# Both stages in one program: attention of the first images inside the convolution's last image, and a token stage on pairs of images

## The reference, cut to what matters

```python
def reference(x, ...):                      # x: (8, 16, 16, 64), float32
    x = x + deformable_conv(group_norm(x))  # 8 groups, 9 taps, bilinear samples, then out @ op_w
    t = x.reshape(8, 256, 64)               # tokens
    n = layer_norm(t)
    q, k, v = n @ Wq.T + bq, n @ Wk.T + bk, n @ Wv.T + bv
    t = t + softmax(q @ k.T / 8) @ v        # within an image
    n = layer_norm(t)
    g = softmax(n @ gate_w + gate_b)        # 16 experts, the two largest kept, made to sum to 1
    y = [(silu(n @ w1[e]) * (n @ w2[e])) @ w3[e] for e in range(16)]   # 64 -> 128 -> 64
    return t + sum(g[e] * y[e] for e in range(16))
```

## Time and profile before

| | us |
|---|---|
| median of 3 runs | 456.4 (455.93 to 458.94) |
| the profiled execution's own time | 459.05 |
| its span, first to last instruction | 457.2 |
| PE at work in the span | 410.0 |
| DVE | 335.2 |
| ACT | 259.5 |
| POOL | 141.3 |

### The profile page before, as it was taken

The page is one execution under the profiler, slowest core; times in us unless marked ns, Lnnn a source line. Parts: engine busy times, 40 slices in busy tenths (PEclk is TensorE's granted clock), DMA queues, the critical chain, the costliest instruction groups (busy, mean ns, idle before and its releaser), DMA issues. The chain is left out here.

```text
span 457.2 us, 9731 instructions
## 1 busy us (share of the span) xinstructions
PE 410.0 (90%) x3276; PEld 232.0 (51%) x3276; DVE 335.2 (73%) x730; ACT 259.5 (57%) x571; POOL 141.3 (31%) x172
## 2 busy tenths in 40 slices
PE   1689999999999999999998457989999999999995
PEld 0543343433534335343332345867677776767663
DVE  3479967789777897777889346768777686868652
ACT  2683645746457464574610154676767677685752
POOL 2263223243232422324200164123242333324322
PEclk9979999999999999999999655799999999999997
DMA  8068886938559385583860330000000000000000
GB/s 258 3 155 218 215 222 148 229 89 227 163 122 231 91 226 158 117 239 86 226 162 1 141 134 0 2 0 2 2 0 14 3 0 14 1 2 1 11 3 11
DMA packets 28409, 44.91 MB, mean 98 GB/s; under 512 B 6864, under 2 KB 11088, under 8 KB 27984
## 3 DMA queue, kind: packets, MB, share of 16 engines
q1 hardware_dynamic: 28368, 44.39, 37.6%
HBM read 6.11 MB, written 0.52 MB: 15 GB/s over the span
## 5 line engine op out<-in xcount | busy, mean ns | idle before, releaser
L663 DVE TENSOR_TENSOR prod<-ps_t,a_rep 128x1024 f32<-128x1024 f32 x128 | 152.0, 1219 | 34.5 <-PE ps_t L363 32.3
L363 PE MATMUL ps_t<-b,vt 32*128 32x512 f32 x512 | 74.7, 650 | 1.9 <-DVE prod L663 1.9
L769 POOL TENSOR_TENSOR a<-a,mask 128x512 f32<-128x512 f32 (+1 forms) x40 | 47.0, 1178 | 83.7 <-ACT a L523 81.4
L383 PE MATMUL ps_d<-prod,keep 128*32 128x512 f32 x512 | 69.0, 611 | 0.3 <-DVE prod L663 0.2
L1223 POOL TENSOR_TENSOR total<-total,share 128x256 f32<-128x256 f32 x56 | 40.9, 730 | 86.9 <-DVE share L1117 86.5
L304 PEld LDWEIGHTS ps_m<-om_r,sel 128*128 128x128 f32 x193 | 29.0, 187 | 75.3 <-ACT mask L501 28.2
L1101 DVE TENSOR_TENSOR hidden<-ps_h,gated 128x256 f32<-128x256 f32 x128 | 51.4, 415 | 3.7 <-ACT gated L1316 2.8
L1316 ACT ACTIVATE gated<-ps_h 128x256 f32<-128x256 f32 x128 | 47.8, 387 | 7.5 <-PE ps_h L1436 1.1
L304 PE MATMUL ps_m<-om_r,sel 128*128 128x256 f32 x193 | 49.3, 334 | 0.0
L1117 DVE TENSOR_TENSOR share<-ps_yf,factor 128x256 f32<-128x256 f32 x56 | 23.7, 423 | 30.4 <-issue 12.8
L1310 ACT ACTIVATE factor<-ps_yf 128x256 f32<-128x256 f32 x64 | 24.6, 385 | 37.3 <-PE ps_yf L1471 37.3
(11 more groups left out here) (151 smaller groups left out, 671.3 us busy)
## 6 DMA issues: line engine op xcount, KB each, us to landing
a_rep<-a SPq DMA_DIRECT2D x128, 256.0 KB, 4.7
a_rep<-a SPq DMA_DIRECT2D x32, 128.0 KB, 2.8
w_f<-in_w SPq DMA_DIRECT2D x2, 1024.0 KB, 5.8
start<-in_start SPq DMA_DIRECT2D x1, 1344.0 KB, 7.8
x_turned<-in_x_turned SPq DMA_DIRECT2D x1, 512.0 KB, 3.8
t_tok<-in_x SPq DMA_DIRECT2D x1, 512.0 KB, 9.4
w<-in_w SPq DMA_DIRECT2D x1, 512.0 KB, 7.6
select_f<-in_select SPq DMA_DIRECT2D x1, 512.0 KB, 8.4
```

The source lines that it names most:

```text
L363: mm = pe.matmul(out, vt[par][r, v % 2, :, :, :].rearrange("p j y c -> p (j y c)"), b[par][r, pair_taps(v // 2), :].rearrange("p t x -> p ...
L383: mm = pe.matmul(ps_d[r, :], fold[:, v % 2, :], p, start=v == 0, stop=False, skip_group_check=True)
L663: dve.tensor_tensor(p[:, :, :], t[:, :, :], a_rep[par][:, ms, pair_taps(v // 2), :].rearrange("p m t x -> p m (t x)"), ALU.mult).then_inc( ...
L769: pool.tensor_tensor(v, v, mask[(PAIRS * par + k) % 2][:, 0:wide, :], ALU.mult).then_inc(a_done, 1)
```

## The change

- One function, one block: the SBUF of the convolution that is free before its last image (`early`) is given to the tokens' tiles, and the expert weights are loaded there. `early_free(eng)` stands before that on SP, ACT, DVE and POOL.
- The last image's `sample` and `weight` use two double banks of `ps_t` instead of three (`ring=2`); the third is `ps_bc`.
- Each engine calls `tokens(at, half)` twice per batch of the last image and twice per duet. It runs the steps due there: `due` gives the couple `c` (two images, 512 tokens) whose first place is `first` for couple 0 and `8 (c - 1) + later` for the others. Places -10 to -2 are the batches of the last image, -1 what follows them, 0 to 31 the duets.
- Expert passes have 512 columns: 32 duets, four couples. `expert_output` adds eight duets up in PSUM (`ps_y`). The shares are no longer spread by a matmul: `portions` (DVE) to `turn_portions` (PE) to `copy_portions` (ACT), then `share_out` on SP writes them to DRAM and reads them back with 128 copies (`factor`, four transfers of 1 MB per couple). POOL multiplies them into the output of `silu` (`weigh`), and DVE's `hide` comes after it.
- The first layer norm's last step moves from DVE to ACT (`apply_norm`), and `turn_sum` is four transposes, followed by two additions.

Core of the diff:

```diff
+def due(at, half, first, later):
+    for c in range(COUPLES):
+        if (at, half) == (first if c == 0 else (DUETS * (c - 1) + later[0], later[1])):
+            return c
+    return None
...
+        def early_free(eng):
+            eng.wait_ge(weighted, WPI * (IMAGES - 1))
+            eng.wait_ge(b_done, PAIRS * (IMAGES - 1) + FIRST_B)
+            eng.wait_ge(vt_ready, IMAGES)
+            for halves in a_filled:
+                for half in halves:
+                    eng.wait_ge(half, 16 * 2 * IMAGES)
...
+        LAST_JOBS = [("om", 0), ("om", 1), ("rep", 0), ("out", 0)]
+        LAST_JOBS += [("rep", r) for r in range(1, len(REPS))] + [("turn", 0)]
...
+            early_free(sp)
+            for w, name, arrived in ((w_f[0], "w1", w1_in), (w_f[1], "w2", w2_in), (w3, "w3", w3_in)):
+                sp.dma_start(w[:, :, :], d[name].rearrange("p (e h) -> p e h", e=EXPERTS)).then_inc(arrived, 16)
+            def share_out(c):
+                sp.wait_ge(p_copied, c + 1)
+                sp.dma_start(board[c], dispatch[:, :]).then_inc(p_out, 16)
...
+                if c > 1:
+                    sp.wait_ge(weighed, EXPERTS * (c - 1))
+                sp.wait_ge(p_out, 16 * (c + 1))
+                for g in range(4):
+                    e = slice(PIECE * g, PIECE * (g + 1))
+                    sp.dma_start(factor[c % 2][g], board[c, e].unsqueeze(0).broadcast_to([P, PIECE, WIDE]))\
+                      .then_inc(factor_in[g], 16)
...
-            def sample(v, i, par):
+            def sample(v, i, par, ring=TRING):
...
-                if positive(WPI * i + 2 * v - 1):
-                    pe.wait_ge(weighted, WPI * i + 2 * v - 1)
+                ahead = 0 if ring == 2 and v else 1
+                if positive(WPI * i + 2 * v - ahead):
+                    pe.wait_ge(weighted, WPI * i + 2 * v - ahead)
...
+            def product_1(u):
...
+                if u < 2:
+                    pe.wait_ge(weighted, WPI * IMAGES)
+                else:
+                    pe.wait_ge(silu_done, u - 1)
+                for w, first in ((w_h[0], True), (w_l[0], False)):
+                    mm = pe.matmul(ps_h1[u % 2][:, :], w[:, e, :], xf[c % 2][:, :], start=first, stop=not first)
...
+            def product_2(u):
...
+                    pe.wait_ge(hidden_done, u - 1)
...
+            def expert_output(p):
...
+                pe.wait_ge(hidden_done, 2 * (p + 1))
+                for k in range(2):
+                    u = 2 * p + k
+                    mm = pe.matmul(ps_y[64 * k:64 * k + 64, :], w3[:, u % EXPERTS, :], hidden[u % 4][:, :],
+                                   start=p % DUETS == 0, stop=p % DUETS == DUETS - 1, skip_group_check=True)
...
+            image(IMAGES - 2, 0, SLABS - 1, LAST_JOBS)
+            for v in range(BATCHES):
+                sample(v, IMAGES - 1, 1, 2)
+                tokens(v - PLACES, "X")
+                if v >= LAG:
+                    reduce(v - LAG, IMAGES - 1, 1)
+                else:
+                    reduce(BATCHES + v - LAG, IMAGES - 2, 0)
+                tokens(v - PLACES, "Y")
+            tokens(-1, "X")
+            reduce(BATCHES - 1, IMAGES - 1, 1)
+            tokens(-1, "Y")
+            product_1(0)
+            for p in range(DUETS * COUPLES):
+                product_1(2 * p + 1)
+                product_2(2 * p)
+                tokens(p, "X")
+                if 2 * p + 2 < UNITS:
+                    product_1(2 * p + 2)
+                product_2(2 * p + 1)
+                tokens(p, "Y")
+                if p:
+                    expert_output(p - 1)
...
+            silu(0)
+            for p in range(DUETS * COUPLES):
+                silu(2 * p + 1)
+                tokens(p, "A")
+                if 2 * p + 2 < UNITS:
+                    silu(2 * p + 2)
+                tokens(p, "B")
...
+            early_free(dve)
+            for v in range(BATCHES):
+                weight(2 * v, IMAGES - 1, 1, 2)
+                tokens(v - PLACES, "A")
+                weight(2 * v + 1, IMAGES - 1, 1, 2)
+                tokens(v - PLACES, "B")
+            tokens(-1, "A")
+            tokens(-1, "B")
+            for p in range(DUETS * COUPLES):
+                if p:
+                    hide(2 * p - 1)
+                tokens(p, "A")
+                hide(2 * p)
+                tokens(p, "B")
...
+            def weigh(u):
+                c, e = u // EXPERTS, u % EXPERTS
+                if e % PIECE == 0:
+                    pool.wait_ge(factor_in[e // PIECE], 16 * (c + 1))
+                pool.wait_ge(silu_done, u + 1)
+                pool.tensor_tensor(gated[u % 4][:, :], gated[u % 4][:, :], factor[c % 2][e // PIECE][:, e % PIECE, :],
+                                   ALU.mult).then_inc(weighed, 1)
```

1425 lines of the change are left out of this document (690 added, 735 removed).

## The result

| | before | after |
|---|---|---|
| median of the runs (us) | 457.5 (455.93 to 458.94, 4 runs) | 466.0 (465.56 to 470.79, 4 runs) |
| ratio, 95% interval | | 1.021 (1.013 to 1.029) |
| span of the profiled execution | 457.2 | 464.2 |
| PE at work in it | 410.0 | 394.3 |

The account below looks back on a forecast made before the run. PE and DVE bound the convolution, waits the handover, PE the products. 303.7 + 89.4 + 19.5 (attention) + 18 + 2 + 2 + 3 + 5.4 = 443 us span, 444.9 executed, less 2.65 to the median: 442 us, range 416 to 464.

Parts of the forecast that it names:

- Start of the last image: Wait for all replicas ahead of the last image: DVE starts at 236 instead of 230, +6 us, bounds 0 and 8.
- Last image with attention inside: Last image's convolution: 37 us of DVE work plus 14 of waits, stage end at 287, bounds 273 and 300.
- Gate ahead of the products: First trip of the shares through DRAM after 287: shares there at 299, second pair of hidden rows at 303.7.
- rival C: Transfers of the shares land late, first quarter at 9 to 12 us instead of 4.8: 465 us, chance 0.13.
- Products: Expert products: 32 duets of 2.9 us, 93 us, 89.4 left after the eight half units done; POOL, DVE, ACT hidden.
- transitions 18: Three later couples' borders: PE waits 5.6 to 6.3 us each for the shares, 18 us in all, bounds 6 and 35.
- exps 2: Product stage: three blocks of gate exps on ACT cost 0.6 us each beyond PE's lead, 2 us.
- DVE steps 2: Product stage: DVE steps of 1.5 us ahead of a duet's second `hide` cost 2 us.
- tail of 5.4: From the last duet's output to the last instruction: copy, four transposes, two additions and a store, 5.4 us.
- three stops of 5.6 to 6.3 us: Sign at the couples' borders: three PE stops of 5 to 6 us, ended by POOL or DVE after a DMA wait.
- Falling clock after the stops: 3: Product stage: slower PE clock after the stops at the couples' borders costs 3 us.
- Rival B: Clock stays at 0.50 through much of the last image and after each stop: +8 to 15, 454 us, chance 0.15.

Follow-up runs that it names:

- e1: Changed kernel with the shares of couples 1 to 3 not fetched through DRAM (couple 0's used instead): 463.7 us, 1.007 of before.
- e3: Changed kernel with a couple's exps in one block on ACT, gate exps behind attention exps, top two half a duet later: 466.7 us, 1.018 of before.
- e5: Changed kernel with idle matmuls on PE, 34 at the first border and 22 at each later one: 476.8 us, 1.040 of before.
- e7: Changed kernel with the share of a couple's first expert as a transfer of its own (256 KB): 466.7 us, 1.019 of before.
- e9: Changed kernel with silu replaced by a plain copy, so that ACT changes no table: 460.8 us (456.0, 465.6), no ratio.
- e15: Changed kernel with only the portions turned and copied earlier: 466.5 us, 1.018 of before.
- e4: Changed kernel with the attention steps of places -10 to -1 behind the last image instead of inside it: 493.2 us, 1.076 of before.
- e16: Changed kernel with only the order of steps changed as in e14, without the later early_free and small first transfer: 441.5 us, 0.966 of before.
- e14: e13 with the exps block, top two, portions and maximum of the scores earlier for couples 1 to 3: 431.6 us, 0.945 of before.
- e6: Changed kernel without shares: DVE takes the output of silu, POOL's products and the DRAM trips are gone: 442.6 us, 0.967 of before.
- e12: e11 with v copied ahead of the low parts, portions turned ahead of attention weights and copied half a duet earlier: 447.9 us, 0.978 of before.
- e11: Changed kernel with a later early_free wait and the edits of e3 and e7: 455.6 us, 0.997 of before.
- e13: e12 with the gate exps ahead of the attention exps inside ACT's block: 440.0 us, 0.959 of before.
- e10: e6 with silu also replaced by a plain copy, so neither shares nor table changes: 430.0 us, 0.939 of before.
- e17: Order of e14 and its later early_free, but shares of couples 1 to 3 not sent through DRAM: 432.4 us, 0.944 of before.
- e18: e14 with eight stops added, PE waiting in every fourth duet for DVE: 450.2 us (443.0 to 451.3), no ratio.

## Why the prediction was wrong

By its own steps:

- *Start of the last image*: right (235.3 for 236, DVE idle 5.87 for 6).
- *Last image with attention inside*: right in this profile (stage end 288 for 287), and lucky. In the six other profiles of the same code up to there (e1, e3, e5, e7, e9, e15) DVE starts at 237.1 to 238.9 and the last residual is done at 292.8 to 296.3. e4 shows that the overlap pays 27 us.
- *Gate ahead of the products*: right (301.3 for 299; `hide` at 302.6 where I had the second pair at 303.7). The first quarters landed in 4.4 to 4.6 us for 4.8. So rival C, whose 465 us is nearly the measured time, is refuted as a mechanism: the transfers came at 420 GB/s and on time.
- *Products*: POOL 1.28, `hide` 0.69, `silu` 0.60 as forecast. The duet is 3.05 us, not 2.9: 32 x 0.15 = 4.8 us missed.
- *Waits*: transitions 18, exps 2, DVE steps 2. Together 22 of idle time, 27.4 with a tail of 5.4; from 305.8 on 23.8 were measured. Within it the trips were sized too high (three stops of 5.6 to 6.3 us were to be the sign; PE's stops for `hidden` at the borders are 2.75, none and 3.59) and the rest too low: the stops at `v_tok`, at the exps and at the copies inside a couple, which I had walked through for the last image and not for the product stage.
- ***Falling clock after the stops: 3***. This is the step that failed. PE has 136.7 us at work where the same 532 records take 119.5 in e16 and 120.1 in e14: the clock costs 17 us, not 3. I had priced it once, for the stops at the borders, while PE has five stops of 1.2 to 2.1 us between 322 and 353 us alone. Several edits that removed idle time took about as much again or more off PE's time at work (e1 6.0 and 6.8; e6 9.1 and 8.8), but there is no fixed rate: e12 took 6.8 us off the idle time of e11 and 0.8 off its work, e13 then 0.1 and 8.1.

The span missed by 21.2 us: 2.1 ahead of the second `hide`, 19.1 behind it. There PE is at work for 134.6 us in after and 117.4 in e16, where the forecast has 108.9 (89.4 and 19.5) and 3 for the clock. So the clock missed by 14.2; the work itself by 8.5, of which 4.8 are the duets and the rest the attention steps and the tail; and the idle time was 3.6 shorter than forecast. *Rival B* had the clock as its mechanism, at 0.15 and 454 us, in the last image and after each stop. Its second half is what happened in this profile; its first half shows in the six others, where the stage up to the first `hide` ran at 0.72 to 0.79 instead of 0.84 and ended 6 to 10.5 us later. The Trainium skill, "TensorE: Matmul & The Clock Gate", Why this matters for your kernels, with its advice against idle gaps between bursts of matmuls, agrees in kind with these 17 us. Of the other page of the Trainium skill weighed ahead, "ScalarE: Activation LUTs", What ACT_TABLE_LOAD costs: by its 2.66 us the ten loads of the stage would be 27 us, an estimate from that page; e9 gives 8.2 and e10 13.3 for them, and a load stands in the trace with 1.28 us, so the measurements decide for the trace's figure. My 2 us was too low by a factor of four or more all the same; I had counted only the gate exps beyond PE's lead and not that the copy of the portions queues behind the loads.

What stood behind the clock is the written order. e16 changed places alone: 161.6 to 134.8 us in the stage, 466.0 to 441.5 in all. That is shown, and so is that with the new order the trips are worth less than 4 us (e17). The chain between them is read from the traces and only argued: the copy that starts the trip was the last item behind a block of ACT of 10 us; stops of PE followed, at the trip's end and inside the couples; these lowered the clock; and at the lower clock PE caught up late, into the next block. Which of the moves of e16 is worth what stays open: e15, the portions alone, left the total at 466.5. Which rule makes the clock fall behind one stop and not behind another of the same length stays open too (e13 against e12: the same idle time, clock 0.97 against 0.89; e18's two stops). That the clock alone, with the stops as they were, would have made the forecast right is only argued from PE's time at work; e5, which tried to hold it, added work of its own, and e13 comes nearest: 8.1 us less at work with the idle time of e12.

## What to carry to other kernels

When a handover in the middle of a full stage begins on an in-order engine, look first at what is queued ahead of the instruction that starts it: here moving some eight steps on PE, ACT and DVE, most of them by half a duet to one duet, turned 2% slower into 3% faster (5.5% with two smaller edits), and the transfer of 4.4 to 4.6 us behind it didn't need to become shorter. Price short stops of PE twice, as idle time and as slow matmuls behind them; here the second part was 17 us beside 25, at no fixed rate per stop. And take the table loads of ACT at their full length where no other wait covers them (e10).

## What was not expected of the hardware

- Behind stops of 1.58 and 1.17 us the clock fell to the 1.2 GHz level (0.58 in 350 to 356), and elsewhere PE stayed there though busy (10.70 of 12 us at 0.50 in 386 to 398), while in e18 a stop of 3.47 us was passed at 1.00.
- A source of 32 KB in DRAM read by 128 partitions came at 420 GB/s, as fast as the distinct data of the expert weights did before; 256 KB of it landed in 3.7 to 3.8 us, 1 MB in 4.4 to 4.6.
- With 34 idle matmuls at the first stop the clock was 1.00 for 18 us instead of 0.50, and the couple's time did not change: 46.4 us for 46.6, at a mean clock of 0.85 in both.
- The same code ahead of the first `hide` took 73.2 us at a clock of 0.84 in one profile and 80.7 at 0.71 in another.
